# Four column quarters, group ends on TensorE and ScalarE, and a result made in quarters of 128 columns

## The chip, the cores and the metric

One core of a Trainium2 chip runs the whole kernel. The metric is the device time of one execution in microseconds (us); the median of the runs is used. All data is fp32. The engines are TensorE (PE; its weight loads are listed apart as PEld), VectorE (DVE), ScalarE (ACT), GpSimd (POOL) and SyncE (SP), whose queue issues all transfers here.

## The reference

A small conditional adapter: for each of 4 samples, two weight matrices are made from a vector `h` of 128 numbers, and then used on 1024 rows of `x`.

```python
# x (4, 1024, 512), h (4, 128); Wd (128, 512), Wu (512, 128); Wdd, Wdu (65536, 128)
dWd = ((h @ Wdd.T + bdd) * 0.1).reshape(B, 128, 512)
dWu = ((h @ Wdu.T + bdu) * 0.1).reshape(B, 512, 128)
Wd_b = Wd + dWd
Wu_b = Wu + dWu
down = relu(einsum('bld,bnd->bln', x, Wd_b) + bd)
up = einsum('bln,bdn->bld', down, Wu_b) + bu
return x + up
```

Wdd and Wdu are 33.5 MB each and are read once; x and the result are 8.4 MB each.

## The kernel before

**Chunks and groups.** Wdd and then Wdu are read in 32 chunks each of 2048 rows (1 MB), through a ring `w` of four. DVE transposes a chunk in 32x32 blocks into a ring `wt` of four (L240), in two instructions of 1024 elements a partition, each with a semaphore of its own, so that the matmuls can begin on the front half. TensorE multiplies it with `st`, a zero-filled pattern of `h` (`sum_chunk`, L406 to L417): four fp32 matmuls of 64 stationary columns and 512 moving ones, which go alternately to the lower and the upper 64 partitions of `acc`. Each fp32 matmul is two instructions in the trace. Four chunks make a group. A group ends so: ACT copies `acc` to `g_rows` with the factor 0.1 (`copy_group`, L324), TensorE transposes that in four steps into `gt` (`turn_group`, L425), and DVE adds the two halves and the base weights into `wd_b` or `wu_b` in two additions (`add_group`, L246 and L248). The eight groups of Wdd are "down" groups, those of Wdu "up" groups. Wd is transposed once on TensorE for `base_d` (L440, L334), Wu for `base_u` (L508, L368).

**The first stage** (loops `turn`) handles Wdd. **The second stage** (loop over `t` from 0 to 31, each engine has its own) handles Wdu, and each step t carries a share of the work on x. At t below 16 TensorE transposes x (`turn_x` twice, L458) into a ring of four banks; ACT copies them to `xt` (L349), POOL adds `bu` to x (L393). At t from 3 to 18 one `down_unit` (L468; eight instructions of 256 columns) computes 256 rows, and ACT applies bias and relu (L357, `copy_down`). From t = 19 on an `up_unit` (L481) multiplies two row tiles with 256 columns of `wu_b` into a bank, and DVE adds it to x two steps later (`finish_unit`, L290, `UP_LAG`), ahead of the next chunk's transpose in program order.

**Order.** The order on each engine is that of the program text. In a step TensorE does the chunk's sum, then at t % 4 = 1 `turn_group` for the group before, then `turn_x`, `down_unit`, `up_unit`. ACT does at t % 4 = 1 `copy_group`, then the copies of x, then `copy_down`. The left half (columns 0 to 255) of the result needs up groups 0 to 3 and is made in 16 units inside t = 19 to 31; the right half needs all groups and is made in 16 units after the last group has been added. SP loads a chunk when the one four before it is transposed; the stores (`store`, L186) lie between loads and after them.

Of the kernel before, what the change touches and what calls it, by code (L numbers as in the profile page):

```python
# [5 lines left out]
P = 128  # L6
QUAD = 32
# [18 lines left out]
FILL = SLOTS * (PART + Q * B)  # L26
FILL_STEP = PART + Q * B
# [11 lines left out]
HALF = D // 2  # L39
UP_I = 2  # L40
UP_UNITS = B * I // UP_I

# [3 lines left out]
UP_START = 19  # L46
UP_AT = {}
_v = 0
for _t in range(UP_START, CHUNKS):
    _n = 2 if _t % 4 == 2 else 1  # L50
    UP_AT[_t] = list(range(_v, min(_v + _n, UP_UNITS)))
    _v += _n
assert _v >= UP_UNITS
# [10 lines left out]
def hyper_adapter(nc, x, cond, Wd, bd, Wu, bu, Wdd, bdd, Wdu, bdu, out):  # L64
# [10 lines left out]
    with ctx:  # L75
# [17 lines left out]
        base_d = sb("base_d", [P, C, N])  # L93
        base_u = sb("base_u", [P, D])
# [9 lines left out]
        nat = [down[:, b, 0:C, :] for b in range(B)]  # L104
        wd_nat, bdd_nat, wu_nat, bdu_nat = nat
# [4 lines left out]
        bank = [pb(f"bank{n}", [P, UP_I * HALF]) for n in range(BANK_RING)]  # L110
# [13 lines left out]
        base_summed = sem("base_summed")  # L124
        base_turned = sem("base_turned")
        base_ready = sem("base_ready")
        wt_front_ready = sem("wt_front_ready")
        wt_ready = sem("wt_ready")
        chunk_summed = sem("chunk_summed")
        g_ready = sem("g_ready")  # L130
        g_turned = sem("g_turned")
        part1_added = sem("part1_added")
        group_added = sem("group_added")
# [11 lines left out]
        def unit_at(v):  # L145

            return v // UP_UNITS, v % UP_UNITS // (I // UP_I), v % (I // UP_I) * UP_I

        def unit_x(v):
            half, b, i0 = unit_at(v)  # L150
            return xs[:, b, i0:i0 + UP_I, half * HALF:(half + 1) * HALF]

        @block.sync
        def _(sp):
# [9 lines left out]
            def turn(it):  # L164
                for u in range(TURN_CHUNKS):
                    c = TURN_CHUNKS * it + u
                    load_chunk(c, wdd_chunks[c], u % W_RING)
                    if u == 1 and isinstance(it, int):
                        load_base_d()

            def load_base_d():
                sp.dma_start(wd_nat, Wd.rearrange("n (c d) -> n c d", c=C)).then_inc(base_d_loaded, 16)
                sp.dma_start(bdd_nat, bdd.rearrange("(n c d) -> n c d", c=C, d=P)).then_inc(base_d_loaded, 16)  # L173

            def load_base_u():
                sp.dma_start(wu_nat, Wu.rearrange("(c d) n -> d c n", c=C)).then_inc(base_u_loaded, 16)
                sp.dma_start(bdu_nat, bdu.rearrange("(c d n) -> d c n", c=C, n=N)).then_inc(base_u_loaded, 16)
                sp.dma_start(bu_all[:], bu.rearrange("(o d) -> o d", o=1).to_broadcast([P, D])
                             ).then_inc(base_u_loaded, 16)
                sp.dma_start(bd_col[:], bd.rearrange("(p o) -> p o", o=1)).then_inc(base_u_loaded, 16)  # L180

            def store(v, units):
                half, b, i0 = unit_at(v)
                i0 -= (units - 1) * UP_I
                sp.wait_ge(unit_final, v + 1)
                sp.dma_start(out_rows[b, :, i0:i0 + units * UP_I, half * HALF:(half + 1) * HALF],  # L186
                             xs[:, b, i0:i0 + units * UP_I, half * HALF:(half + 1) * HALF]
# [8 lines left out]
            at = {t: v for t, units in UP_AT.items() for v in units if v % 4 == 3}  # L196
            for t in range(CHUNKS):
# [4 lines left out]
                load_chunk(CHUNKS + t, wdu_chunks[t], t % W_RING)  # L202
                if t - UP_LAG - W_RING - 1 in at:
                    store(at.pop(t - UP_LAG - W_RING - 1), 4)
                    stores += 1
            for t in sorted(at):
                store(at[t], 4)
                stores += 1
            for v in range(UP_UNITS + 1, 2 * UP_UNITS - 2, 2):
                store(v, 2)  # L210
                stores += 1
            for v in range(2 * UP_UNITS - 2, 2 * UP_UNITS):
# [5 lines left out]
        def _(dve):  # L218
# [9 lines left out]
            for q in range(Q):  # L228
                rows = slice(QUAD * q, QUAD * (q + 1))
                place = st[rows].rearrange("p r (s z) -> p r s z", z=FILL_STEP)[:, :, :, q * B:(q + 1) * B]  # L230
                nc.vector.tensor_copy(place, h32[rows].unsqueeze(2).to_broadcast([QUAD, R, SLOTS, B])
                                      ).then_inc(st_ready, 1)

            def transpose(c, slot, tslot, loaded):
                dve.wait_ge(w_loaded[slot], loaded)
                if later(c, T_RING):
                    dve.wait_ge(chunk_summed, c - T_RING + 1)
                chunk = w[:, slot, :].rearrange("p (k r h) -> p k r h", r=R, h=QUAD)
                for r, ready in ((0, wt_front_ready), (R // 2, wt_ready)):
                    nc.vector.transpose(wt[:, tslot, r:r + R // 2].rearrange("p r (k j) -> p k r j", j=QUAD),  # L240
                                        chunk[:, :, r:r + R // 2]).then_inc(ready, 1)

            def add_group(g, parts, base, total):

                dve.wait_ge(g_turned, g + 1)
                nc.vector.tensor_tensor(total, parts[1], base, ALU.add).then_inc(part1_added, 1)  # L246
                dve.wait_ge(part1_added, g + 1)
                nc.vector.tensor_tensor(total, parts[0], total, ALU.add).then_inc(group_added, 1)  # L248

            def turned_parts():  # L250
                v = gt[:].rearrange("p c (a s b) -> p c a s b", s=SQ, b=B)
                return [v[:, :, a] for a in range(2)]

            def add_down_group(g):
                n = bass.ds(g * SQ, SQ)
                total = wd_b[:, :, :, n].rearrange("p c b s -> p c s b")
                base = base_d[:, :, n].unsqueeze(3).to_broadcast([P, C, SQ, B])
                add_group(g, turned_parts(), base, total)

            def add_up_group(g):  # L260
                d = slice((g - GROUPS) * D // GROUPS, (g - GROUPS + 1) * D // GROUPS)
                total = wu_b[:, :, d].rearrange("p b (s c) -> p c s b", c=C)
                base = base_u[:, d].rearrange("p (s c) -> p c s", c=C)
                add_group(g, turned_parts(), base.unsqueeze(3).to_broadcast([P, C, SQ, B]), total)

            def turn(it):
                for u in range(TURN_CHUNKS):
                    c = TURN_CHUNKS * it + u
                    transpose(c, u % W_RING, u % T_RING, 16 * (2 * it + u // W_RING + 1))
                    if u == 3 and isinstance(it, int):  # L270

                        dve.wait_ge(base_d_loaded, 16 * 2)
                        nc.vector.scalar_tensor_tensor(wd_nat, bdd_nat, DELTA_SCALE, wd_nat,
                                                       ALU.mult, ALU.add).then_inc(base_summed, 1)
                    if u == 3 and not isinstance(it, int):
                        add_down_group(2 * it - 1)
                    if u == SLOTS + 3:
                        if isinstance(it, int):
                            dve.wait_ge(base_ready, 1)
                        add_down_group(2 * it)  # L280
# [5 lines left out]
            def finish_unit(v):  # L286
                place = unit_x(v)
                dve.wait_ge(bu_added, v % UP_UNITS + 1)
                dve.wait_ge(up_summed, v + 1)
                nc.vector.tensor_tensor(place, bank[v % BANK_RING][:].rearrange("p (i d) -> p i d", d=HALF),  # L290
                                        place, ALU.add).then_inc(unit_final, 1)

            for t in range(CHUNKS):
                c = CHUNKS + t
                transpose(c, t % W_RING, t % T_RING, 16 * (c // W_RING + 1))
                if t == 2:
                    dve.wait_ge(base_u_loaded, 16 * 4)
                    nc.vector.scalar_tensor_tensor(wu_nat, bdu_nat, DELTA_SCALE, wu_nat,
                                                   ALU.mult, ALU.add).then_inc(base_summed, 1)
                if t == 2 * SLOTS - 1:  # L300
                    dve.wait_ge(base_ready, 2)
                if t % SLOTS == 3:

                    g = c // SLOTS - 1
                    add_down_group(g) if g < GROUPS else add_up_group(g)
# [3 lines left out]
            for t in range(CHUNKS, CHUNKS + UP_LAG):  # L309
                if t == CHUNKS + UP_LAG - 1:  # L310
                    add_up_group(2 * GROUPS - 1)
                for v in UP_AT.get(t - UP_LAG, ()):
                    finish_unit(v)
            for v in range(UP_UNITS, 2 * UP_UNITS):
# [3 lines left out]
        def _(act):  # L318
            def copy_group(g, n):

                act.wait_ge(chunk_summed, SLOTS * (g + 1))
# [5 lines left out]

            def turn(it):
                for u in range(TURN_CHUNKS):
                    if u == 1 and not isinstance(it, int):  # L330
                        copy_group(2 * it - 1, 1)
                    if u == 5 and isinstance(it, int):
                        act.wait_ge(base_turned, 1)
                        nc.scalar.activation(base_d[:], bank[0][:].rearrange("p (c n) -> p c n", c=C),  # L334
                                             ACT.Copy).then_inc(base_ready, 1)
                    if u == SLOTS + 1:
                        copy_group(2 * it, 0)
# [23 lines left out]
            for t in range(CHUNKS):  # L361
# [4 lines left out]
                if t == SLOTS + 1:  # L366
                    act.wait_ge(base_turned, 2)
                    nc.scalar.activation(base_u[:], gt[:].rearrange("p c n -> p (c n)"), ACT.Copy  # L368
                                         ).then_inc(base_ready, 1)
# [7 lines left out]
            copy_group(2 * GROUPS - 1, 1)  # L377

        @block.gpsimd
        def _(pool):  # L380
# [8 lines left out]
            bu_pair = bu_all[:].unsqueeze(1).to_broadcast([P, UP_I, D])  # L389
# [149 lines left out]
```

## Time and profile before

| | |
|---|---|
| median of 3 runs | 245.08 us (244.66 to 245.51) |
| the profiled execution's own time | 245.09 us |
| its span in the trace | 243.2 us |
| PE busy | 215.1 us, 88% |
| DVE busy | 189.4 us, 78% |
| ACT, POOL busy | 34.9 us, 39.8 us |
| bytes moved | 85.35 MB, mean 351 GB/s |

The span runs from the first to the last record of the profiled execution; what lies around it is 245.09 - 243.2 = 1.9 us. A share of busy time is a mean over stages with different limits, so the stages have to be read one by one.

### The profile page before, as it was taken

How to read it: one execution, taken by the hardware profiler on the slowest of the kernel's cores; microseconds unless marked ns; L12 is line 12 of the kernel's file. 1: busy time of each engine (PE TensorE's matmuls, PEld its weight loads, DVE VectorE, ACT ScalarE, POOL GpSimd, SP SyncE). 2: the span in 40 equal slices, each digit the busy share in tenths (PEclk: the TensorE clock that was granted, in tenths of full speed). 3: DMA queues.
4: the chain of work that ended last, by engine and by line, in shares of the span. 5: the costliest groups of instructions: out<-in, count | busy, mean ns of one | idle time of the engine just before them, and what ended most of it. 6: DMA issues, size and time to landing. Idle time of an engine off the chain costs nothing.

```text
span 243.2 us, 2728 instructions
## 1 busy us (share of the span) xinstructions
PE 215.1 (88%) x972; PEld 98.0 (40%) x972; DVE 189.4 (78%) x200; ACT 34.9 (14%) x67; POOL 39.8 (16%) x23
## 2 busy tenths in 40 slices
PE   0798797878979796989999999999999999997991
PEld 0213121212212122446556655665644535354881
DVE  2799999899999994887377775295178999985782
ACT  2001000000000000412442333324110000000000
POOL 2000000000000000666444553465000000000000
PEclk9999999999999997999999999999999999999998
DMA  5999999999999999999999999949335889950897
GB/s 220 426 420 425 426 415 422 420 419 391 377 350 425 426 410 384 426 416 423 423 420 423 416 423 416 410 168 388 163 147 222 327 268 360 386 191 0 286 337 242
DMA packets 20419, 85.35 MB, mean 351 GB/s; under 512 B 1588, under 2 KB 10808, under 8 KB 11192
## 3 DMA queue, kind: packets, MB, share of 16 engines
q1 hardware_dynamic: 20408, 85.21, 88.6%
q8 instruction: 7, 0.11, 0.2%
q14 instruction: 4, 0.03, 0.0%
HBM read 76.81 MB, written 8.39 MB: 350 GB/s over the span
## 4 chain that ended last, share of the span: by engine, by line
PE 52%; DVE 19%; DMA 17%; issue 6%; ACT 2%; SPq 1%; DVEq 0%; ACTq 0%
PE acc L414 21%; DVE wt L240 17%; PE bank L481 12%; PE dn L468 12%; DMA w<-in_L_cond_Wdd_dram 11%; DMA w<-in_L_cond_Wdu_dram 6%; PE bank L458 5%; PE gt L425 2%; DVE wd_b L246 1%; ACT xt L349 1%; SPq L158 1%; ACT g_rows L324 1%; ACT down L357 0%; SPq L173 0%; DVE xs L290 0%
## 5 line engine op out<-in xcount | busy, mean ns | idle before, releaser
L240 DVE STREAM_TRANSPOSE wt<-w 128x1024 f32<-128x1024 f32 x128 | 149.2, 1214 | 25.4 <-DMA w<-in_L_cond_Wdu_dram 19.8
L414 PE MATMUL acc<-wt,st 128*64 128x512 f32 x512 | 132.1, 624 | 18.2 <-DVE wt L240 16.6
L414 PEld LDWEIGHTS acc<-wt,st 128*64 128x64 f32 x512 | 29.6, 138 | 96.0 <-DVE wt L240 60.8
L393 POOL TENSOR_TENSOR xs<-xs,bu_all 128x1024 f32<-128x1024 f32 x16 | 38.0, 2377 | 128.9 <-PE bank L458 128.9
L481 PE MATMUL bank<-wu_b,down 128*128 128x256 f32 x128 | 31.1, 388 | 1.4 <-DVE wu_b L248 1.4
L468 PE MATMUL dn<-xt,wd_b 128*128 128x256 f32 x128 | 30.5, 381 | 0.0
L481 PEld LDWEIGHTS bank<-wu_b,down 128*128 128x128 f32 x128 | 23.2, 190 | 12.3 <-issue 5.7
L290 DVE TENSOR_TENSOR xs<-bank,xs 128x512 f32<-128x512 f32 x32 | 21.7, 681 | 7.3 <-PE bank L481 7.3
L349 ACT ACTIVATE xt<-bank 128x512 f32<-128x512 f32 x32 | 17.5, 594 | 64.5 <-PE dn L468 44.0
L468 PEld LDWEIGHTS dn<-xt,wd_b 128*128 128x128 f32 x128 | 23.1, 190 | 4.1 <-issue 1.6
L324 ACT ACTIVATE g_rows<-acc 128x512 f32<-128x512 f32 x16 | 9.6, 599 | 93.2 <-PE acc L414 93.2
L458 PEld LDWEIGHTS bank<-ident,xs 128*128 128x128 f32 x128 | 14.6, 146 | 10.5 <-issue 10.5
L458 PE MATMUL bank<-ident,xs 128*128 128x128 f32 x128 | 18.0, 285 | 0.0
L246 DVE TENSOR_TENSOR wu_b<-gt,base_u 128x256 f32<-128x256 f32 x8 | 4.8, 603 | 13.4 <-PE gt L425 13.4
L425 PEld LDWEIGHTS gt<-ident,g_rows 128*128 128x128 f32 x64 | 6.8, 141 | 13.2 <-issue 8.1
L425 PE MATMUL gt<-ident,g_rows 128*128 128x128 f32 x64 | 10.5, 286 | 0.7 <-ACT g_rows L324 0.4
L357 ACT ACTIVATE down<-dn,bd_col 128x256 f32<-128x256 f32 x16 | 7.6, 477 | 8.8 <-PE dn L468 8.8
L248 DVE TENSOR_TENSOR wu_b<-gt,wu_b 128x256 f32<-128x256 f32 x8 | 4.9, 617 | 0.3
L248 DVE TENSOR_TENSOR wd_b<-gt,wd_b 128x256 f32 (+1 forms) x8 | 4.9, 612 | 0.3
L246 DVE TENSOR_TENSOR wd_b<-gt,base_d 128x256 f32 (+1 forms) x8 | 4.6, 570 | 0.0
L334 ACT ACTIVATE base_d<-bank 128x512 f32<-128x512 f32 x1 | 0.6, 599 | 19.8 <-PE bank L440 19.8
L402 PE MATMUL gt<-ident,xt 4*128 4x4 f32 x4 | 0.6, 248 | 2.9 <-DVE xt L221 2.9
(19 smaller groups left out, 9.5 us busy)
## 6 DMA issues: line engine op xcount, KB each, us to landing
w<-in_L_cond_Wdd_dram SPq DMA_DIRECT2D x32, 1024.0 KB, 7.3
w<-in_L_cond_Wdu_dram SPq DMA_DIRECT2D x32, 1024.0 KB, 10.0
xs<-in_x_dram SPq DMA_DIRECT2D x8, 1024.0 KB, 14.6
out_dram<-xs SPq DMA_DIRECT2D x4, 1024.0 KB, 7.1
out_dram<-xs SPq DMA_DIRECT2D x7, 512.0 KB, 3.9
out_dram<-xs SPq DMA_DIRECT2D x2, 256.0 KB, 3.6
down<-in_L_cond_Wd_dram SPq DMA_DIRECT2D x1, 256.0 KB, 7.1
down<-in_L_cond_bdd_dram SPq DMA_DIRECT2D x1, 256.0 KB, 7.3
```

Source lines behind the costliest of these rows:

```text
L240: nc.vector.transpose(wt[:, tslot, r:r + R // 2].rearrange("p r (k j) -> p k r j", j=QUAD), chunk[:, :, r:r + R // 2]).then_inc(ready, 1)
L246: nc.vector.tensor_tensor(total, parts[1], base, ALU.add).then_inc(part1_added, 1)
L248: nc.vector.tensor_tensor(total, parts[0], total, ALU.add).then_inc(group_added, 1)
L290: nc.vector.tensor_tensor(place, bank[v % BANK_RING][:].rearrange("p (i d) -> p i d", d=HALF), place, ALU.add).then_inc(unit_final, 1)
L324: nc.scalar.activation(g_rows[:, n].rearrange("p (j k) -> p j k", k=K), acc[n][:].rearrange("p (k j) -> p j k", k=K), ACT.Copy, scale=DELT ...
L349: nc.scalar.activation(xt[:, j % XT_RING, c0:c0 + BANK_C, :], bank[m % BANK_RING][:].rearrange("p (c l) -> p c l", c=BANK_C), ACT.Copy).th ...
L393: nc.gpsimd.tensor_tensor(xs[:, b, i0:i0 + UNIT_I], xs[:, b, i0:i0 + UNIT_I], bu_pair, ALU.add).then_inc(bu_added, 1)
L414: last = nc.tensor.matmul(a[PART * part:PART * (part + 1)], st[:, r, s * PART:(s + 1) * PART], wt[:, slot, r], start=s == 0 and r < 2, sto ...
L425: last = nc.tensor.transpose(gt[:, k], g_rows[:, n, k * P:(k + 1) * P], ident[:])
L458: last = nc.tensor.transpose(bank[m % BANK_RING][:, n * P:(n + 1) * P], xs[:, b, i0 + i, c * P:(c + 1) * P], ident[:])
L468: last = nc.tensor.matmul(dn[:], wd_b[:, c, j // BATCH_UNITS], xt[:, j % XT_RING, c], start=c == 0, stop=c == C - 1)
L481: last = nc.tensor.matmul(bank[v % BANK_RING][:, i * HALF:(i + 1) * HALF], down[:, b, i0 + i], wu_b[:, b, half * HALF:(half + 1) * HALF], ...
```

## The change

- `sum_chunk` becomes `sum_pair`: `st` has 32 columns instead of 64, and the matmuls of two chunks (4 x 2, of 512 moving columns each) go in turn to four strips of 32 partitions of `acc`. TensorE waits for both chunks of a pair; DVE's transpose waits for a pair, too. The transpose of a chunk is one instruction of 2048 elements.
- A group's end leaves DVE. `turn_group` is now four times two accumulating fp32 matmuls with 64 moving columns: `g_rows` against `fold` (two identities added, which sums the two parts), and the base weights against a repeated slice of the identity. ACT copies `gt` to `wd_b` or `wu_b` (`store_group`), right behind `copy_group` in its order. The separate transposes of Wd and Wu and their copies go; Wd is read with whole rows of 2 KB.
- The result is made in quarters of 128 columns. A unit is four row tiles of 128 columns (same bank size). Quarter 0 runs at t = 16 to 19, two units a step; quarter 1 at t = 20 to 27, one a step; quarter 2 at t = 28 to 31, two a step; quarter 3, eight units, after the last group. Stores follow; their rows are 512 bytes.
- Chunks are read in the order 0, 2, 1, 3 within a group.

```diff
+PAIR = 2
+TILE = 32
+FILL = PAIR * (TILE + Q * B)
+FILL_STEP = TILE + Q * B
+ORDER = (0, 2, 1, 3)
...
-HALF = D // 2
-UP_I = 2
-UP_UNITS = B * I // UP_I
+QUARTERS = 4
+QD = D // QUARTERS
+UP_I = 4
+BATCH_UPS = I // UP_I
+UP_UNITS = B * BATCH_UPS
+ALL_UPS = QUARTERS * UP_UNITS
...
-UP_START = 19
...
+UP_AT = {16 + n: [2 * n, 2 * n + 1] for n in range(4)}
+UP_AT |= {20 + n: [UP_UNITS + n] for n in range(8)}
+UP_AT |= {28 + n: [2 * UP_UNITS + 2 * n, 2 * UP_UNITS + 2 * n + 1] for n in range(4)}
...
             def transpose(c, pair, slot, tslot, loaded):
                 dve.wait_ge(w_loaded[slot], loaded)
                 if later(c, T_RING):
+                    dve.wait_ge(pair_summed, pair - T_RING // PAIR + 1)
+                nc.vector.transpose(wt[:, tslot].rearrange("p r (k j) -> p k r j", j=QUAD),
+                                    w[:, slot, :].rearrange("p (k r h) -> p k r h", r=R, h=QUAD)
+                                    ).then_inc(wt_ready, 1)
...
+            def store_group(g, total):
+
+                act.wait_ge(g_turned, g + 1)
+                nc.scalar.activation(total, gt[:, :, 0:PART].rearrange("p c (s b) -> p c s b", b=B), ACT.Copy
+                                     ).then_inc(group_ready, 1)
...
                     copy_group(g, g % 2)
...
+                    down_group(g) if g < GROUPS else up_group(g)
...
+            def sum_pair(c, low, slot, a):
+
+                pe.wait_ge(wt_ready, c + PAIR)
                 for r in range(R):
+                    for h in range(PAIR):
+                        place = 2 * (r % 2) + h
+                        last = nc.tensor.matmul(a[TILE * place:TILE * (place + 1)],
+                                                st[:, r, low * TILE:(low + 1) * TILE], wt[:, slot + h, r],
+                                                start=low == 0 and r < 2, stop=low == 1 and r >= 2)
+                last.then_inc(pair_summed, 1)
+
+            def turn_group(g, n, base, select):
 
                 pe.wait_ge(g_ready, g + 1)
                 if later(g, 1):
+                    pe.wait_ge(group_ready, g)
                 for k in range(C):
-                    last = nc.tensor.transpose(gt[:, k], g_rows[:, n, k * P:(k + 1) * P], ident[:])
+                    nc.tensor.matmul(gt[:, k, 0:PART], g_rows[:, n, k * P:(k + 1) * P], fold[:],
+                                     start=True, stop=False)
+                    last = nc.tensor.matmul(gt[:, k, 0:PART], base(k),
+                                            select(k).unsqueeze(2).to_broadcast([P, SQ, B]),
+                                            start=False, stop=True)
                 last.then_inc(g_turned, 1)
...
             def up_unit(v):
-                half, b, i0 = unit_at(v)
-                pe.wait_ge(group_added, GROUPS + (half + 1) * GROUPS // 2)
+                quarter, b, i0 = unit_at(v)
+                pe.wait_ge(group_ready, GROUPS + (quarter + 1) * GROUPS // QUARTERS)
...
-                sum_chunk(c, s, t % T_RING, acc[n][:])
+                if s % PAIR == 0:
+                    sum_pair(c, s // PAIR, t % T_RING, acc[n][:])
```

## Rows read from the trace of the kernel before

**Rows 1.** The page: engines' busy time, transfer rate in 40 slices of 6.1 us.
```profile
PE 215.1 (88%) x972; PEld 98.0 (40%) x972; DVE 189.4 (78%) x200; ACT 34.9 (14%) x67; POOL 39.8 (16%) x23
GB/s 220 426 420 425 426 415 422 420 419 391 377 350 425 426 410 384 426 416 423 423 420 423 416 423 416 410 168 388 163 147 222 327 268 360 386 191 0 286 337 242
```

**Rows 2.** Stretches: from:to, length; busy time of PE, PEld, DVE, ACT, POOL; PEclk, DMA share, GB/s.
```profile
70.00:80.00 10.00, 8.51 (x38) 2.09 (x36) 9.97 (x11) 0.60 (x1) 0.00 (x0) 1.00 1.00 422
120.00:130.00 10.00, 10.00 (x54) 6.13 (x52) 7.85 (x8) 2.90 (x6) 5.49 (x3) 1.00 1.02 425
190.00:200.00 10.00, 10.00 (x44) 4.39 (x42) 9.99 (x12) 0.60 (x1) 0.00 (x0) 1.00 0.81 276
```

**Rows 3.** Groups with shapes: line, engine, out<-in, count | busy us, mean ns | idle before.
```profile
L240 DVE STREAM_TRANSPOSE wt<-w 128x1024 f32<-128x1024 f32 x128 | 149.2, 1214 | 25.4 <-DMA w<-in_L_cond_Wdu_dram 19.8 <-DMA w<-in_L_cond_Wdd_dram 3.6 <-PE acc L414 1.1
L246 DVE TENSOR_TENSOR wu_b<-gt,base_u 128x256 f32<-128x256 f32 x8 | 4.8, 603 | 13.4 <-PE gt L425 13.4
```

**Rows 4.** DVE in order of time: start, us, instructions [idle before]; start of Wdd's middle and of stage two.
```profile
49.69 9.13 DVE L240 STREAM_TRANSPOSE wt<-w 128x1024 f32<-128x1024 f32 x8
59.87 2.36 DVE L240 STREAM_TRANSPOSE wt<-w 128x1024 f32<-128x1024 f32 x2
...
91.95 2.37 DVE L240 STREAM_TRANSPOSE wt<-w 128x1024 f32<-128x1024 f32 x2 [1.29 <-DMA w<-in_L_cond_Wdu_dram]
111.85 4.86 DVE L240 STREAM_TRANSPOSE wt<-w 128x1024 f32<-128x1024 f32 x4 [1.66 <-DMA w<-in_L_cond_Wdu_dram]
```

**Rows 5.** The chain that ended last, in order of time: start, us, what.
```profile
110.65 1.87 PE acc L414 x8
112.52 1.02 PE bank L458 x8
113.54 1.74 PE dn L468 x8
...
117.85 0.66 PE gt L425 x4
118.51 0.87 PE bank L458 x8
...
137.71 0.87 PE bank L458 x8
...
168.77 1.87 PE acc L414 x8
170.64 1.92 PE dn L468 x8
...
182.41 1.06 PE bank L481 x4
...
188.85 0.86 PE bank L481 x4
...
224.16 14.09 PE bank L481 x64
...
238.35 0.69 DVE xs L290
```

**Rows 6.** The first weight loads of the last burst, two narrow windows: start, union of times, count.
```profile
224.16 0.19 PEld L481 LDWEIGHTS bank<-wu_b,down 128*128 128x128 f32 x1 [1.59 <-DVE wu_b L248]
224.16 0.30 PEld L481 LDWEIGHTS bank<-wu_b,down 128*128 128x128 f32 x2 [1.59 <-DVE wu_b L248]
```

**Rows 7.** ACT beside TensorE around t = 17, in order of time: start, us, instruction.
```profile
172.60 0.47 ACT L357 ACTIVATE down<-dn,bd_col 128x256 f32<-128x256 f32 x1 [2.28 <-PE dn L468]
172.97 0.59 ACT L324 ACTIVATE g_rows<-acc 128x512 f32<-128x512 f32 x1
```

**Rows 8.** Stretches as in rows 2: rates of 512-byte and 1 KB rows, and the clock.
```profile
91.00:92.00 1.00, 0.00 (x0) 0.00 (x0) 0.04 (x1) 0.00 (x0) 0.00 (x0) 1.00 1.12 308
95.00:96.00 1.00, 1.00 (x4) 0.00 (x0) 0.00 (x0) 0.00 (x0) 0.00 (x0) 0.50 0.99 410
230.00:232.00 2.00, 2.00 (x11) 1.77 (x10) 1.66 (x3) 0.00 (x0) 0.00 (x0) 1.00 1.02 345
```

More of the change, by code:

```diff
@@ L102, in hyper_adapter @@
         cond_rep = xt[0:B, 0, 1:3, :].rearrange("b c (r q i) -> b (c r) q i", q=Q, i=QUAD)
-        nat = [down[:, b, 0:C, :] for b in range(B)]
-        wd_nat, bdd_nat, wu_nat, bdu_nat = nat
+        bdd_nat = down[:, 0, 0:C, :].rearrange("p c n -> p (c n)")
+        bdu_nat = down[:, 1, 0:C, :]
         acc = [pb(f"acc{n}", [P, COLS]) for n in range(2)]
@@ L201, in _ @@
                     load_base_u()
[L202 to L209, printed above, removed]
+                load_chunk(CHUNKS + t, wdu_chunks[t // SLOTS * SLOTS + ORDER[t % SLOTS]], t % W_RING)
+                for v in UP_AT.get(t - UP_LAG - W_RING - 1, ()):
+                    if v % BATCH_UPS == BATCH_UPS - 1:
+                        store(v, BATCH_UPS)
+                        stores += 1
+            for t in range(CHUNKS - UP_LAG - W_RING - 1, CHUNKS):
+                for v in UP_AT.get(t, ()):
+                    if v % BATCH_UPS == BATCH_UPS - 1:
+                        store(v, BATCH_UPS)
+                        stores += 1
+            for v in range(ALL_UPS - UP_UNITS + 1, ALL_UPS - 2, 2):
                 store(v, 2)
                 stores += 1
-            for v in range(2 * UP_UNITS - 2, 2 * UP_UNITS):
+            for v in range(ALL_UPS - 2, ALL_UPS):
                 store(v, 1)
@@ L230, in _, with transpose @@
                 place = st[rows].rearrange("p r (s z) -> p r s z", z=FILL_STEP)[:, :, :, q * B:(q + 1) * B]
-                nc.vector.tensor_copy(place, h32[rows].unsqueeze(2).to_broadcast([QUAD, R, SLOTS, B])
+                nc.vector.tensor_copy(place, h32[rows].unsqueeze(2).to_broadcast([QUAD, R, PAIR, B])
                                       ).then_inc(st_ready, 1)
-            def transpose(c, slot, tslot, loaded):
+            def transpose(c, pair, slot, tslot, loaded):
                 dve.wait_ge(w_loaded[slot], loaded)
@@ L236, in transpose @@
                 if later(c, T_RING):
[L237 to L248, printed above, removed]
@@ L326, in copy_group, with down_group, up_group @@
                                      ACT.Copy, scale=DELTA_SCALE).then_inc(g_ready, 1)
-            def turn(it):
[L329 to L337, printed above, removed]
+            def store_group(g, total):
+                act.wait_ge(g_turned, g + 1)
+                nc.scalar.activation(total, gt[:, :, 0:PART].rearrange("p c (s b) -> p c s b", b=B), ACT.Copy
+                                     ).then_inc(group_ready, 1)
+            def down_group(g):
+                store_group(g, wd_b[:, :, :, bass.ds(g * SQ, SQ)].rearrange("p c b s -> p c s b"))
+            def up_group(g):
+                d = slice((g - GROUPS) * D // GROUPS, (g - GROUPS + 1) * D // GROUPS)
+                store_group(g, wu_b[:, :, d].rearrange("p b (s c) -> p c s b", c=C))
+            def turn(it):
+                for n in range(2):
+                    if n == 1 or not isinstance(it, int):
+                        copy_group(2 * it + n - 1, 1 - n)
+                        down_group(2 * it + n - 1)
             turn(0)
@@ L377, in _ @@
             copy_group(2 * GROUPS - 1, 1)
+            up_group(2 * GROUPS - 1)
         @block.gpsimd
@@ L404, in _ @@
             last.then_inc(cond_turned, 1)
-            def sum_chunk(c, s, slot, a):
-                pe.wait_ge(wt_front_ready, c + 1)
+            def sum_pair(c, low, slot, a):
+                pe.wait_ge(wt_ready, c + PAIR)
                 for r in range(R):
-                    if r == R // 2:
-                        pe.wait_ge(wt_ready, c + 1)
-                    part = r % 2
-                    last = nc.tensor.matmul(a[PART * part:PART * (part + 1)],
-                                            st[:, r, s * PART:(s + 1) * PART], wt[:, slot, r],
-                                            start=s == 0 and r < 2, stop=s == SLOTS - 1 and r >= 2)
-                last.then_inc(chunk_summed, 1)
@@ new lines, in turn_group, with turn_down_group, turn_up_group @@
+                    last = nc.tensor.matmul(gt[:, k, 0:PART], base(k),
+                                            select(k).unsqueeze(2).to_broadcast([P, SQ, B]),
+                                            start=False, stop=True)
+                last.then_inc(g_turned, 1)
+            def turn_down_group(g, n):
+                turn_group(g, n, lambda k: base_d[:, k * P:(k + 1) * P],
+                           lambda k: ident[:, bass.ds(g * SQ, SQ)])
+            def turn_up_group(g):
+                first = (g - GROUPS) * D // GROUPS
+                row = first % P
+                pick = ident[:, row:row + D // GROUPS].rearrange("p (s c) -> p c s", c=C)
+                turn_group(g, g % 2, lambda k: base_u[:, first // P], lambda k: pick[:, k])
@@ L434, in turn @@
                         pe.wait_ge(g_ready, 2 * it + n - 1)
-                    sum_chunk(c, s, u % T_RING, acc[n][:])
-                    if u == 4 and isinstance(it, int):
-                        pe.wait_ge(base_summed, 1)
-                        for k in range(C):
-                            last = nc.tensor.transpose(bank[0][:, k * P:(k + 1) * P], wd_nat[:, k], ident[:])
-                        last.then_inc(base_turned, 1)
+                    if s % PAIR == 0:
+                        sum_pair(c, s // PAIR, u % T_RING, acc[n][:])
                     if u == 1 and not isinstance(it, int):
-                        turn_group(2 * it - 1, 1)
+                        turn_down_group(2 * it - 1, 1)
                     if u == SLOTS + 1:
-                        turn_group(2 * it, 0)
+                        if isinstance(it, int):
+                            pe.wait_ge(fold_ready, 1)
+                            pe.wait_ge(base_d_summed, 1)
+                        turn_down_group(2 * it, 0)
             turn(0)
@@ L480, in up_unit @@
                 for i in range(UP_I):
-                    last = nc.tensor.matmul(bank[v % BANK_RING][:, i * HALF:(i + 1) * HALF],
-                                            down[:, b, i0 + i], wu_b[:, b, half * HALF:(half + 1) * HALF],
+                    last = nc.tensor.matmul(bank[v % BANK_RING][:, i * QD:(i + 1) * QD],
+                                            down[:, b, i0 + i], wu_b[:, b, quarter * QD:(quarter + 1) * QD],
                                             start=True, stop=True)
@@ L502, in _ @@
                     up_unit(v)
-                if t == SLOTS:
-                    pe.wait_ge(base_summed, 2)
-                    pe.wait_ge(group_added, GROUPS)
-                    for k in range(C):
-                        last = nc.tensor.transpose(gt[:, k], wu_nat[:, k], ident[:])
-                    last.then_inc(base_turned, 1)
-            turn_group(2 * GROUPS - 1, 1)
-            for v in range(UP_UNITS, 2 * UP_UNITS):
+            turn_up_group(2 * GROUPS - 1)
+            for v in range(ALL_UPS - UP_UNITS, ALL_UPS):
                 up_unit(v)
```

115 lines of the change are left out of this document (38 added, 77 removed).

## The prediction

> **What bounds the kernel now.** I read the page's busy shares and slices first [rows 1], then stretches of the span, because shares mix stages [rows 2], then the groups by shape for durations [rows 3], and last DVE in order of time and the chain of waits for cadences [rows 4, 5]. Three stages show. In the first (to about 90 us) DVE is busy 9.97 of 10 us and TensorE waits for it; four chunks take 59.87 - 49.69 = 10.2 us on DVE, transposes and two additions together, while four chunks at 422 GB/s are 4.19 MB / 422 = 9.9 us [rows 2, 4]. DVE is just ahead of the transfers as the limit. In the second stage, from about 107 us, TensorE is busy 10.00 of 10 us [rows 2]: a step with x costs 1.87 (sum) + 1.02 + 1.74 = 4.63 us, and four steps with a group's end 137.71 - 118.51 = 19.2 us [rows 5]. Up to some 155 us the transfers run at 416 to 425 GB/s beside it and then fall [rows 1], so they are the second limit there. From 182 to 222 us TensorE and DVE are both full [rows 2]. The third stage is the right half: 14.09 us of matmuls, then 0.69 us of DVE, then 243.2 - 239.04 = 4.16 us until the last store is in [rows 5].
>
> **Sum of a pair.** Eight instructions of 512 columns take 1.87 us two at a time, so one round of two is 1.87 / 4 = 0.47 us [rows 5]. A pair has 16 instructions; four at a time that is four rounds, 1.87 us again, against 3.74 before. No row shows four strips at once. Bounds: 1.87 (each strip adds no time, as the second does) and 3.74 (only two at a time). I take 1.87, because the two that run at once in the trace have separate moving data too. The Trainium skill (TensorE: Matmul & The Clock Gate, Part 3) says that three column tiles measured 2.38 times one; scaled to four it would make an estimated pair of 2.2 us and add 0.3 us for each pair on the path. No row shows three.
>
> **Transpose and the group's end.** One transpose of 2048 elements in place of two of 1024: from the cadence, eight instructions in 9.13 us are 2.28 us a chunk [rows 4]; I take 2.3 with its handoff, bounds 2.1 and 2.4. DVE loses 2 x 0.6 us a group [rows 3]. On TensorE a group's end grows from 0.66 us to 16 weight loads with short matmuls. The second weight load of a burst starts 0.30 - 0.19 = 0.11 us after the first [rows 6], so I take 16 x 0.108 = 1.73 us, +1.07; bounds 0.9 (half that pitch) and 3.0 (0.19, the whole record, each). ACT's copy of 256 elements is like L357, 0.47 us [rows 7]; it is on the path only at the last group.
>
> **First stage.** With DVE at 4 x 2.3 = 9.2 us a group the transfers bind at 9.9. Before chunk 0 of Wdu come 34.5 MB of 1.049 MB: 36.2 / 0.422 = 85.7 us behind a start of 3.7 gives 89.4, against 91.95 [rows 4]: -2.5 us, bounds 0 and -2.5. TensorE's longer group end is covered by its idle time: 2 x 1.87 + 1.73 = 5.5 us in 9.9.
>
> **Second stage, t to 15.** Chunk t = 5 began on DVE at 111.85 after a wait for its transfer [rows 4]; 2.5 earlier and 2.3 of transpose put the pair of t = 4 at 111.7 on TensorE. From there TensorE binds. Four steps cost 19.2 less 2 x 1.87 (half their sums) and 1.07 more, and there is a stall that is new. At t % 4 = 1 TensorE did a sum of 1.87 us ahead of `turn_group`; now it goes straight to it, and waits for `copy_group`, which stands behind `copy_down` of the step before on ACT. From the end of the down matmuls (170.64 + 1.92 = 172.56) to the end of L324 (172.97 + 0.59) is 1.0 us [rows 5, 7]. Behind this wait are queued on TensorE the transposes of x and the down unit, for which ACT and POOL wait in turn. So 19.2 - 3.74 + 1.07 + 1.0 = 17.5 us: 111.7 + 3 x 17.5 = 164.2 at t = 16, where the kernel before stood at 168.77 [rows 5]. Transfers: six MB in four steps are 14.9 us, under 17.5.
>
> **t = 16 to 31.** A unit of four tiles is eight pairs of weight load and matmul with 128 columns. Its streaming time is half of 0.22 us each, 14.09 / 64 / 2 = 0.11; the weight loads' pitch is 0.11 too [rows 5, 6]. If both overlap, a unit costs 0.87 us as before [rows 5]. Bounds 0.87 and 8 x 0.19 = 1.52 (the record's length as pitch). I take 0.87, since the loads of `turn_x`, 128 columns as well though in transposes, hide behind 128 moving ones (0.87 for eight [rows 5]). Then t = 16: 1.87 + 1.92 + 1.73 = 5.5; t = 17: 1.1 (the stall with its handoff) + 1.73 + 1.74 + 1.73 = 6.3; t = 18: 5.5, at 181.5. From here a loop binds that no engine shows alone: the units of an even step on TensorE, DVE's `finish_unit` for them (0.69), which stands ahead of the transpose of the odd chunk (2.3), and the pair, which waits for that chunk. With 0.3 of handoffs that is 3.3, and a round of two steps costs 1.87 + 1.06 + 3.3 = 6.3 us; DVE alone needs 2 x (2.3 + 0.69) = 6.0. First pair of t = 20: 184.8; four rounds to t = 28: 210.0. t = 28 and 29: 3.8 + 1.73 + 1.73 = 7.3; t = 30 and 31: 3.8 + 1.7; at 222.8. Group end 1.73, ACT 0.6, handoff 0.1: 225.2.
>
> **The tail.** Eight units 8 x 0.87 + 0.2 = 7.2, DVE 0.7, last store 4.2 + 0.3: 237.6. The 0.3 is for rows of 512 bytes: the nearest stretch, with loads of such rows, has 308 GB/s, against 345 for rows of 1 KB in the stores [rows 8]; 256 KB take 0.85 us at the lower rate, so the stores just keep up with the units. Bounds 0 and +3 (a rate of about 200).
>
> **Sum.** 237.6 - 243.2 = -5.6: the tail gives -7.0, the start of the tail +1.0, the stores +0.3, rounded. With 1.9 us around the span the time is 239.5 us; the profiled execution, 245.09, stands at the median of the runs, 245.08.
>
> **Rivals.**
> 1. Slower: weight loads set the pace of the quarter units, as half the columns lie between two loads. Place: 8 units at t = 16 to 19, 4 on the loop's path at t = 20 to 27, 8 at t = 28 to 31, 8 in the tail: 28. At 0.19 us a pair a unit costs 0.65 more, +18.2, so 257.7. It decides from +0.2 a unit, 0.135 us a pair, on. For it: the record is 0.19 us long. Against: the pitch of 0.11 [rows 6]. The Trainium skill (TensorE: Matmul & The Clock Gate, Back-to-back issue gap) has 81 ns for a stream of load and matmul at 128 columns where matmuls alone have 56, a rule that speaks against these units; 25 ns more a pair would be an estimated +0.2 a unit and +5.6 in all, near no change. Chance 0.15, spread from 245 up.
> 2. Slower: only two strips run at once. A pair stays at 3.74 and the steps have gained +1.07 and the stall: 2 pairs in each of 3 rounds before t = 16, then 2, 4 and 2 pairs on the path are 14 x 1.87 = 26.2, so 265.7. Against it speaks that two do run at once. Chance 0.05.
> 3. The clock. TensorE had 0.50 at 95 us after the one long idle stretch around 91 [rows 8]; that is 1.2 GHz in place of 2.4. TensorE will idle in 2 to 3 us pieces throughout stage one and in the loop of t = 20 to 27. In stage one a doubled 5.5 us is 11 in 9.9, nearly covered. In the loop it adds up to 1.87 + 1.06 a round, 4 rounds, +11.7: 251. Half of it gives 245. Chance 0.10.
> 4. Better than forecast: the stall on ACT or the handoffs are hidden, 4 x 1.1 less: 235.1. Chance 0.07.
> 5. The gain is eaten by small terms (DVE's finishes, POOL beside DVE, slow stores) and the time stays within 0.3%: 0.05.
>
> **How the numbers follow.** The forecast, 239.5 with 236 to 243.5 around it, has the remaining 0.58. Low 235.5 takes in part of rival 4; high 251 takes in rivals 5, 3 and the lower part of 1. Left out: rival 2, the top of 1, times below 235.5, about 0.18. A measurement of this kernel tells about 0.3% from no change. Faster: 0.58 + 0.07 + 0.03 (mild forms of 1 and 3) = 0.68; same 0.07; slower 0.25.
>
> **What would show it.** Pair: 16 instructions of L414's successor in 1.9 us, or 3.7. Units: eight weight loads at 0.11 or 0.19 pitch; the tail's 64 matmuls in 7.1 us or up to 12. ACT: TensorE idle about 1.1 us ahead of `turn_group` at t = 5, 9, 13, 17. Loop: DVE busy near 10 of 10 us at t = 20 to 27 with rounds of 6.3 us. Stage one: the first chunk of Wdu on DVE at 89.5 us. Clock: 1.00 in the second stage. The forecast fails first if a unit costs over 1.07 us, or if the transfers with their 512-byte rows become the limit behind t = 24.

## The result

| | median us | range, runs | to the kernel before |
|---|---|---|---|
| before | 245.24 | 244.66 to 245.51, 4 | |
| changed | 256.97 | 254.9 to 258.32, 4 | 1.047 (95%: 1.039 to 1.056) |

The change makes the kernel 4.7% slower, where 239.5 us was forecast. The profiled execution of the changed kernel took 254.9 us, with a span of 253.0; it is the fastest of its runs. Every ratio here leaves out runs that took over 1.5% more than the fastest of the same kernel, and every median is over all runs.

The page of the changed kernel, where it answers [rows 1] (with TensorE's granted clock in tenths):

```profile
PE 189.2 (75%) x1284; PEld 117.4 (46%) x1284; DVE 170.2 (67%) x105; ACT 43.9 (17%) x81; POOL 38.7 (15%) x23
PEclk9995978879779795779999679979999999979998
GB/s 231 426 421 420 426 420 420 421 417 426 418 422 425 416 378 424 422 416 426 416 424 421 417 376 210 202 262 57 111 41 291 269 364 382 402 338 157 164 167 249
```

Both full engines lost work, TensorE 26 us and DVE 19 us, and the kernel still got slower: no engine is full any more. The transfer row shows where. From slice 24 to 29 (counted from 0; 152 to 190 us) the transfers are at 41 to 262 GB/s: the loads have run ahead as far as the rings allow and wait for a slot to come free. The kernel before has such a dip too (168, 388, 163, 147 GB/s [rows 1]), but it starts later and is shallower. Most single costs came out as forecast. Groups of the changed kernel, and lines of its chain of waits (start, us, what):

```profile
L244 DVE STREAM_TRANSPOSE wt<-w 128x2048 f32<-128x2048 f32 x64 | 147.4, 2307 | 52.5 <-DMA w<-in_L_cond_Wdu_dram 21.9 <-PE acc L388 21.4 <-DMA w<-in_L_cond_Wdd_dram 8.5
L301 ACT ACTIVATE wu_b<-gt 128x256 f32<-128x256 f32 x8 | 5.1, 635 | 44.6 <-PE gt L401 44.6
```

```profile
182.39 1.78 PE bank L467 x16
184.18 0.17 PE gt L399 x2
...
185.91 1.78 PE dn L454 x8
...
189.47 1.85 PE acc L388 x16
```

A pair's 16 instructions on four strips take 1.85 us, four rounds of 0.46; the sum had 1.87. Two quarter units take 1.78 us, 0.89 each; the sum had 0.87. A group's end takes 185.91 - 184.18 = 1.73 us, as in the sum. DVE's transposes, 2.3 us with the handoff, fit as well. The first chunk of Wdu reached DVE at 90.8 us (89.5 forecast, 91.95 before [rows 4]): less than half of the 2.5 us that the first stage was to give. DVE's idle 21.4 us behind `PE acc` (1.1 before [rows 3]) is the new thing: it stands still because TensorE does not get to its pairs.

The place is t = 9 of the second stage (starts in us; ACT beside TensorE), and the same instructions in stretches (columns as in [rows 2]):

```profile
137.26 1.89 PE L454 MATMUL dn<-xt,wd_b 128*128 128x256 f32 x8
139.25 1.09 ACT L327 ACTIVATE xt<-bank 128x512 f32<-128x512 f32 x2 [3.16 <-PE dn L454]
140.22 0.48 ACT L335 ACTIVATE down<-dn,bd_col 128x256 f32<-128x256 f32 x1
140.57 0.61 ACT L294 ACTIVATE g_rows<-acc 128x512 f32<-128x512 f32 x1
141.24 0.54 PE L399 MATMUL gt<-fold,g_rows 128*128 128x64 f32 x2 [2.08 <-ACT g_rows L294]
...
144.55 1.91 PE L444 MATMUL bank<-ident,xs 128*128 128x128 f32 x8
146.26 2.88 PE L454 MATMUL dn<-xt,wd_b 128*128 128x256 f32 x8
```

```profile
139.20:141.20 2.00, 0.00 (x0) 0.00 (x0) 0.54 (x1) 1.93 (x4) 0.66 (x1) 1.00 1.04 430
141.40:148.20 6.80, 6.80 (x29) 6.44 (x30) 1.58 (x1) 0.63 (x1) 1.65 (x1) 0.50 1.02 422
148.40:151.00 2.60, 2.60 (x21) 0.81 (x20) 0.00 (x0) 1.45 (x3) 0.49 (x1) 1.00 0.92 375
```

After the down unit TensorE is idle for 2 us, while ACT does two copies of x, the relu and the group's copy in a row. ACT's bracket says why the copies of x come so late: they waited 3.16 us for `PE dn`, the down unit itself. The code has it, in `copy_x`: with a ring of three for `xt`, the copies at step t wait for the down unit of step t. And right behind the idle stretch the granted clock is 0.50 (1.2 GHz in place of 2.4) for 6.8 us, in which TensorE is busy all the time at half its pace: the eight transposes of x take 1.91 us in place of 1.04.

### The profile page after: what moved, and what is told of

Its sections match the earlier page's. It is cut to its first block, busy times and chain, and to the rows that moved or that the text cites. A ratio compares the mean times of both kernels' runs of the same rounds, so it can differ in the third digit from the quotient of the medians.

```text
span 253.0 us, 3267 instructions
## 1 busy us (share of the span) xinstructions
PE 189.2 (75%) x1284; PEld 117.4 (46%) x1284; DVE 170.2 (67%) x105; ACT 43.9 (17%) x81; POOL 38.7 (15%) x23
## 4 chain that ended last, share of the span: by engine, by line
PE 45%; DMA 33%; DVE 13%; issue 4%; ACT 3%; SPq 1%; ACTq 0%; DVEq 0%
DMA w<-in_L_cond_Wdd_dram 26%; PE dn L454 12%; DVE wt L244 12%; PE acc L388 11%; PE bank L467 9%; DMA w<-in_L_cond_Wdu_dram 7%; PE bank L444 6%; PE gt L399 3%; PE gt L401 3%; ACT xt L327 1%; DVE xs L268 1%; ACT down L335 1%; SPq L161 1%; ACT g_rows L294 1%; SPq L177 0%
## 5 line engine op out<-in xcount | busy, mean ns | idle before, releaser
L244 DVE STREAM_TRANSPOSE wt<-w 128x2048 f32<-128x2048 f32 x64 | 147.4, 2307 | 52.5 <-DMA w<-in_L_cond_Wdu_dram 21.9
L388 PE MATMUL acc<-wt,st 128*32 128x512 f32 x512 | 78.8, 744 | 45.5 <-DVE wt L244 45.5
L388 PEld LDWEIGHTS acc<-wt,st 128*32 128x32 f32 x512 | 15.7, 125 | 85.6 <-issue 52.2
L467 PE MATMUL bank<-wu_b,down 128*128 128x128 f32 x256 | 31.6, 278 | 0.7 <-ACT wu_b L301 0.7
L399 PE MATMUL gt<-fold,g_rows 128*128 128x64 f32 x128 | 26.4, 290 | 7.5 <-ACT g_rows L294 5.3
L399 PEld LDWEIGHTS gt<-fold,g_rows 128*128 128x128 f32 x128 | 20.7, 204 | 19.7 <-issue 13.2
L401 PE MATMUL gt<-ident,base_u 128*128 128x64 f32 x64 | 13.8, 301 | 0.0
L401 PE MATMUL gt<-ident,base_d 128*128 (+1 forms) x64 | 12.4, 275 | 0.0
L401 PEld LDWEIGHTS gt<-ident,base_u 128*128 128x128 f32 x64 | 11.1, 216 | 0.0
L401 PEld LDWEIGHTS gt<-ident,base_d 128*128 128x128 f32 x64 | 9.8, 193 | 0.0
```

Of the source, the lines that this page charges most:

```text
L244: nc.vector.transpose(wt[:, tslot].rearrange("p r (k j) -> p k r j", j=QUAD), w[:, slot, :].rearrange("p (k r h) -> p k r h", r=R, h=QUAD) ...
L388: last = nc.tensor.matmul(a[TILE * place:TILE * (place + 1)], st[:, r, low * TILE:(low + 1) * TILE], wt[:, slot + h, r], start=low == 0 an ...
L399: nc.tensor.matmul(gt[:, k, 0:PART], g_rows[:, n, k * P:(k + 1) * P], fold[:], start=True, stop=False)
L401: last = nc.tensor.matmul(gt[:, k, 0:PART], base(k), select(k).unsqueeze(2).to_broadcast([P, SQ, B]), start=False, stop=True)
L467: last = nc.tensor.matmul(bank[v % BANK_RING][:, i * QD:(i + 1) * QD], down[:, b, i0 + i], wu_b[:, b, quarter * QD:(quarter + 1) * QD], st ...
```

## The experiments

**Theory A.** At odd steps no sum stands any more between a down unit and what waits for ACT. TensorE is idle 2.1 us at t = 5, 9, 13 and 0.8 us at t = 7, 11, 15, and the longer stretches let the clock fall. (The expectations below count 2.5 us; the trace has 2.13, 2.08 and 2.08.) **Theory B.** The loss comes from the quarters themselves: units of 128 columns, stores with rows of 512 bytes, additions on DVE.

**A ring of four for xt.** One line in the changed kernel.

```diff
-XT_RING = 3
+XT_RING = 4
```

> The changed kernel with a ring of four for xt instead of three, nothing else. Theory A: in the changed kernel ACT's copies of x at step t wait for the down unit of the same step (ring of three), so behind each down unit stand 1.1 us of copies, the relu and at t % 4 = 1 the group's copy; the sum that TensorE did meanwhile at every odd step is gone, and TensorE stands idle 2.5 us at t = 5, 9, 13 and 0.8 us at t = 7, 11, 15; the 2.5 us then let the clock fall to 0.50 (5 us lost). With four buffers the copies run ahead: the idle time at t % 4 = 1 falls to about 1.2 us, that at t % 4 = 3 goes, and the clock holds in t = 5 to 15: 257 - 3 x 1.2 - 3 x 0.8 - 5 = 246 us. Theory B (the 512-byte stores and the quarter units make the loss): no change, 257.

Measured 244.29 us, 12.7 less, against 246 expected; ratio to the kernel before 0.995 (0.991 to 0.999). One extra buffer takes away the whole loss. TensorE's clock is 1.00 from 120 to 190 us. Theory B is out as the main cause. The pairs of t = 4 and t = 16, and the stall at t = 9 between them:

```profile
114.70 1.92 PE L388 MATMUL acc<-wt,st 128*32 128x512 f32 x16
137.94 0.43 PE L399 MATMUL gt<-fold,g_rows 128*128 128x64 f32 x2 [1.05 <-ACT g_rows L294]
167.20 1.92 PE L388 MATMUL acc<-wt,st 128*32 128x512 f32 x16
```

Four steps take (167.20 - 114.70) / 3 = 17.5 us with a stall of 1.05, which are the prediction's own two figures (17.5 and 1.0). So for this stretch the prediction costed the kernel with a ring of four, and not the changed one. Of the 3.8 us by which the profiled run still misses the forecast, 3.0 are the late start of t = 4 (114.7 against 111.7).

**The group's copy two steps earlier**, on ACT; that of the last Wdd group in front of the loop.

```diff
+            copy_group(GROUPS - 1, 1)
             for t in range(CHUNKS):
...
                 if t % SLOTS == 1:
                     g = c // SLOTS - 1
-                    copy_group(g, g % 2)
                     down_group(g) if g < GROUPS else up_group(g)
+                if t % SLOTS == 3:
+                    copy_group(c // SLOTS, c // SLOTS % 2)
...
-            copy_group(2 * GROUPS - 1, 1)
```

> The changed kernel with copy_group moved on ACT two steps earlier, to t % 4 = 3 (that of the last Wdd group in front of the loop); ring of three for xt as before. Theory A: the group's 0.5 us copy and its place behind the relu leave TensorE's path, turn_group starts at once behind the down unit and its 1.8 us cover ACT's copies: idle time at t = 5, 9, 13 falls from 2.5 to 0.3 us, that of 0.8 us at t % 4 = 3 grows to about 1.3; the clock holds: 257 - 6.6 + 1.5 - 5 = 247 us. Theory B: 257.

Measured 242.64 us (0.989; 0.985 to 0.993), 14.3 less, more than the 10 expected. This reaches the same idle stretch from its other end, without a new buffer: `turn_group`'s 1.73 us now stand over most of ACT's copies. The clock is 1.00 from 110 to 210 us here too.

**The clock alone.** Extra matmuls inside the idle time, in front of the wait; nothing uses their result, which the group's matmuls overwrite. They go into `gt` because no PSUM is left for a tile of their own: the first form of this experiment (x3_fill) had one and gave no result.

```diff
-                pe.wait_ge(g_ready, g + 1)
                 if later(g, 1):
                     pe.wait_ge(group_ready, g)
+                if isinstance(g, int) and GROUPS <= g < GROUPS + 3:
+                    for _ in range(4):
+                        nc.tensor.matmul(gt[:, 0:2].rearrange("p c n -> p (c n)"), ident[:],
+                                         base_d[:, 0:UNIT_I * P], start=True, stop=True)
+                pe.wait_ge(g_ready, g + 1)
```

> The changed kernel with four extra matmuls of 256 columns (eight instructions, 1.7 us at the full clock) on TensorE in front of the wait of turn_group for groups 8, 9 and 10 (t = 5, 9, 13), inside its 2.5 us of idle time. They go into gt, which the group's own matmuls then overwrite, and nothing uses them. If the clock falls because of this idle time, it now stays at 1.00 at 141 to 148 and 165 to 169 us, and what these stretches cost, 5 us of the profiled execution, comes back: 252 us against 257. If the clock falls for another reason: 257 to 258.

Measured 249.79 us (1.019; 1.014 to 1.023), 7.2 less than the changed kernel (5 expected), by adding work. The same place in its trace:

```profile
138.47 1.89 PE L399 MATMUL gt<-base_d,ident 128*128 128x256 f32 x8
140.72 0.30 PEld L403 LDWEIGHTS gt<-fold,g_rows 128*128 128x128 f32 x2 [0.76 <-ACT g_rows L294]
...
142.55 1.04 PE L448 MATMUL bank<-ident,xs 128*128 128x128 f32 x8
```

and the stretch behind it (columns as in [rows 2]):

```profile
140.70:148.00 7.30, 7.28 (x56) 5.36 (x57) 2.91 (x2) 2.09 (x4) 2.36 (x1) 1.00 1.02 421
```

The wait for ACT is still there and as long, but TensorE is busy in most of it, and the clock stays at 1.00: 7.28 us now hold 56 matmuls where 6.80 held 29. So the clock is a cause of its own. Of the 14.3 us that the early copy takes away, the clock behind the three stalls makes about half (7.2), the waits themselves the rest.

**Both repairs.** Ring of four and early copy.

> The changed kernel with both: ring of four for xt and copy_group two steps earlier. Theory A: no idle time of ACT's making is left between t = 4 and 16, the clock holds: 257 - 3 x 2.5 - 3 x 0.8 - 5 = 242 us, and one or two less from the start of the stage: 241. Then the loop of finish, transpose and pair (6.3 us for two steps) and the tail are as in the changed kernel. Theory B: 257.

Measured 239.46 us (0.972; 0.963 to 0.980), 17.5 less than the changed kernel, against 241 to 242 expected. TensorE in 16 us of the second stage (the two stretches behind, to 164 us, look the same):

```profile
116.00:132.00 16.00, 16.00 (x113) 11.69 (x112) 9.24 (x4) 7.08 (x14) 9.49 (x4) 1.00 1.01 418
```

The pairs of t = 4 and t = 16 start at 113.6 and 162.1 us: 16.2 us for four steps, without a gap, against 19.2 before and 17.5 in the sum (1.0 of which was a stall). The time is that of the forecast, 239.5, but not by the forecast's terms; the agreement is luck. In the trace t = 4 starts 1.9 us later than in the sum (113.6 against 111.7), the steps to t = 16 take 4.0 less, those to t = 20 0.9 less, the loop 1.0 more (26.2 against 25.2) and the steps from t = 28 on 2.0 more (17.2 against 15.2); the clock falls at t = 24 and t = 28 there, which the fillers below take away.

**Control: the ring of four in the kernel before.**

> The kernel before with a ring of four for xt instead of three. There every step has a sum of 1.87 us between a down unit and what waits for ACT's copies, so the wait on the down unit of the same step cost at most 0.2 us at four steps: no change, 244.5 to 245.2 us. If the ring of three were a cost of its own, as it is in the changed kernel (12.7 us), it would show here too: 233 to 240.

Measured 243.42 us (0.993; 0.991 to 0.996). The ring of three costs the kernel before 1.5 us, more than the expected range allowed, and the changed kernel 12.7.

**The quarters alone**, in the kernel before: constants, steps of the units, stores and `up_unit` as in the changed kernel, the rest untouched.

> The kernel before with the result in quarters of 128 columns alone (units, their steps and the stores as in the changed kernel; sums, group ends and transposes as before). TensorE is full from 107 to 222 us there, so eight units moved from the tail into t = 16 to 31 save 7.1 us at the end and cost 7.1 in the stretch, and DVE gets eight more additions of 0.69 us where it is full as well: 245 to 248 us. If the move itself were the gain: 238. If quarter units or 512-byte stores were slow in themselves: over 250.

Measured 246.66 us (1.005; 1.003 to 1.007), 1.5 us slower than the kernel before in the same comparison. The tail is shorter (13.7 us from its first matmul to the end of the span, against 19.0), but it starts 8.1 us later (232.3 against 224.2): the units moved out of it lengthen a stretch in which TensorE is full.

**The quarters undone**, in the kernel with both repairs: halves of 256 columns from t = 19, sixteen units in the tail, rows of 1 KB.

> Pairs and group ends of the changed kernel, ring of four for xt and copy_group two steps earlier, but the result in halves as in the kernel before (units of 2 x 256 columns from t = 19, sixteen in the tail, stores with rows of 1 KB). The tail is 7.1 us longer, t = 16 to 18 lose six units of 0.89 and t = 28 to 31 three: about 2 us less than 7.1 stay if DVE's loop (6.2 us for two steps) binds as before in t = 20 to 31. So the quarters are worth between 0 and 5 us on top of the pairs: 239.5 to 244.5, at the likeliest 242.

Measured 236.44 us (0.963; 0.956 to 0.970). I expected quarters to be worth up to 5 us; by the medians they cost 3.0. That figure is rough: the four runs of each kernel spread (234.8 to 237.6 against 236.8 to 240.6). With a lag of three, below, the same comparison is clear. The reading behind the expectation was wrong. In the traces halves have their tail 5.9 us longer (18.2 against 12.3), but they reach t = 20 8.0 us earlier (173.8 against 181.8), since TensorE, which is full there, has no eight units of quarter 0 to make. From t = 20 on both kernels take about as long to the tail (42.5 and 43.4 us).

**A lag of three** steps for `finish_unit`, with quarters and with halves.

```diff
-UP_LAG = 2
+UP_LAG = 3
```

> Ring of four for xt and copy_group two steps earlier (239.5 us), and UP_LAG 3 instead of 2: DVE adds a unit three steps after TensorE made it. If the loop of units, finish, transpose and pair binds at t = 20 to 27 (6.2 us for two steps), DVE alone binds then, with 2 x (2.25 + 0.65) = 5.8: 4 to 6 rounds give 2 us, 237.5. If the transfers bind there (342 to 398 GB/s with stores among the loads), no change: 239.5.

> Pairs, group ends, ring of four, copy_group early, the result in halves (236.4 us), and UP_LAG 3. As with quarters (239.5 to 236.1), the finish of a unit no longer stands between it and the next pair's transpose: 2 to 3 us, so 234. If the loop in t = 20 to 31 is bound by other things with halves: 236.4.

Measured 236.08 us (0.959; 0.951 to 0.966) with quarters, 229.27 us (0.934; 0.932 to 0.937) with halves. The loop of finish, transpose and pair is real: without it 3.4 and 7.2 us go (2 and 2 to 3 expected). With halves a part of this is the clock again: with a lag of two TensorE waits 2.3 us for DVE at t = 24 and t = 28 and the pairs behind take 2.91 and 3.46 us in place of 1.85; with a lag of three no pair does. With halves this beats both kernels, by 6.6% and 10.8%. The same two stretches of both kernels, first quarters, then halves:

```profile
190.00:200.00 10.00, 9.10 (x78) 6.11 (x78) 8.69 (x7) 1.24 (x2) 0.00 (x0) 1.00 1.06 376
200.00:210.00 10.00, 6.84 (x36) 3.77 (x35) 8.40 (x7) 0.00 (x0) 0.00 (x0) 0.66 0.95 328
```

```profile
190.00:200.00 10.00, 9.54 (x66) 5.93 (x66) 10.00 (x9) 0.61 (x2) 0.00 (x0) 1.00 0.99 364
200.00:210.00 10.00, 8.84 (x55) 6.35 (x55) 4.80 (x7) 1.84 (x3) 0.00 (x0) 1.00 0.53 178
```

With halves DVE is full and the last transpose ends at 201.3 us. With quarters DVE has gaps at 190 to 210 us. DVE's lines there name what it waits for:

```profile
198.31 2.31 DVE L244 STREAM_TRANSPOSE wt<-w 128x2048 f32<-128x2048 f32 x1 [1.19 <-DMA w<-in_L_cond_Wdu_dram]
205.69 2.31 DVE L244 STREAM_TRANSPOSE wt<-w 128x2048 f32<-128x2048 f32 x1 [1.59 <-DMA w<-in_L_cond_Wdu_dram]
```

The chunks come late there, with stores among the loads, TensorE is idle, and its clock falls (0.66). The 6.8 us between these two kernels are clear of the spread (233.6 to 236.8 against 228.3 to 229.5). How much of them is the 512-byte rows, how much the eight more units and how much the clock, no run separates.

**Filling the loop's gaps.** Extra matmuls, whose result nothing uses, in front of the pair's wait at t = 20 to 28 or 30, once with quarters (lag two), once with halves (lag three).

> Ring of four for xt and copy_group early (239.5 us), with extra matmuls on TensorE in front of the wait for the pair: four of 256 columns (1.7 us) at t = 20, 24, 28, two at t = 22, 26, into the unused half of the bank of dn, once all down units are copied. They compute nothing that is used. If the clock's falls in the loop (3.4 us at 194 and at 208 us in the profile of the kernel without them) cost about 1.8 us each by a slow pair and a slow unit on the loop's path, 3.5 us come back: 236. If the loop is bound by DVE or transfers anyway: 239.5, or more by the extra work.

> As x11, with the extra matmuls in front of the pair's wait at t = 20 to 30 (1.7 us where t % 4 = 0, 0.85 us where it is 2), which compute nothing that is used. If the clock still costs something there, 1 to 3 us come back: 232. If DVE binds with a lag of three, the clock's falls are off the path: as x11, 234, or slower by up to 1.

Measured 236.56 us (0.966; 0.964 to 0.969) against 239.46 without: the clock's falls at t = 24 and t = 28 (pairs of 3.47 and 3.58 us) are gone, and 2.9 us with them, where 3.5 were expected. With halves and a lag of three it was 234.96 us (0.959; 0.957 to 0.962) against 229.27 without: 5.7 us slower. The clock was 1.00 there already and the gaps at most 0.5 us, so the fillers, 7.7 us of them, stood on the path. Filling helps where TensorE waits for long, and costs most of its length where it doesn't.

## Why the prediction was wrong

- **What bounds the kernel now:** right by stages, but the groups of the page were read for durations only. The ACT line of the copies of x, in the page of the kernel before, had the answer in its last column:

```profile
L349 ACT ACTIVATE xt<-bank 128x512 f32<-128x512 f32 x32 | 17.5, 594 | 64.5 <-PE dn L468 44.0
```

- **Sum of a pair, group's end, transposes, units:** right, to 0.02 us a piece (1.85, 1.73, 2.3, 0.89). Rivals 1 and 2 did not come true: a pair of load and matmul takes 1.78 / 16 = 0.11 us, the streaming time alone, so the weight loads hide. The Trainium skill (TensorE: Matmul & The Clock Gate, Back-to-back issue gap) has 81 ns for such a pair where matmuls alone have 56; this trace shows no such surcharge.
- **First stage:** it gave 1.1 us (90.84 against 91.95), within the bounds of 0 and 2.5 but not the 2.5 that the sum used.
- **Second stage, t to 15: the step that failed.** The term of 1.0 us for ACT left out the copies of x, which with a ring of three wait for the down unit of the same step, and the sum put nothing for the clock behind the stalls. The stall at t % 4 = 1 was put at 1.0 us, from the relu and the group's copy. Two copies of x stand in front of them (1.1 us more), and at t % 4 = 3 the same chain delays the next down unit by 0.8 us; the sum had nothing there. TensorE's idle time measured 2.1 and 0.8 us. Without clock effects four steps took 19.6 us, not 17.5. Three rounds make 6.2 us. With a ring of four the same four steps take 17.5.
- **Rival 3, the clock, was named at places that decided less.** It was priced for stage one and for the loop from t = 20. It fell at t = 9 and 13, behind the very stalls the sum had just introduced, for 3.3 and 1.6 us on the path (from pair to pair 14.6 and 12.9 us, where the round without a fall took 11.3), together 4.9. The start of the stage is a further loss: the pair of t = 4 began at 114.9 instead of 111.7 us. Of these 3.2 us, 1.5 are the transfers: chunk t = 5 came to DVE at 110.85 instead of 109.35. The other 1.7 are TensorE's: it had half clock from about 94 to 104 us and again from 108 to 111 (the pairs of t = 0 and t = 2 took 3.64 and 3.15 us) and waited 1.2 us for the group's copy at t = 1; how much of the 1.7 each of the two makes is open. In all 3.2 + 6.2 + 4.9 = 14.3, and t = 16 began at 178.5 us instead of 164.2.
- **The loop from t = 20:** 198.2 to 223.6 us for four rounds, 25.4, against 25.2 forecast. The step at t = 28 met a half clock (pair 3.46 us), +1.9 to the tail. The tail, 240.7 to 253.0, took 12.3 us against 12.4. No stall stood at t = 17, where two units cover it: -0.9. The whole span: 237.6 + 14.3 - 0.9 + 0.2 + 1.9 - 0.1 = 253.0.
- **The stores:** in the tail the transfers ran at 288 GB/s with all engines busy; 308 was used. It cost nothing that shows.
- **The tail's gain is none.** That "the tail gives -7.0" was right, and the terms for t = 16 to 31 were right to 2 us; but the sum never compared quarters against halves with the pairs already in. That comparison is 239.46 against 236.44: the quarters lose 3.0 us, and 6.8 with a lag of three. What the repaired kernels gain on the kernel before comes with the pairs and the group ends; no run separates these two.
- **Range:** 251 was too low because rival 3 and the size of the stall were treated as independent, while the one brings on the other.

## What to carry to other kernels

When work is made faster or moved, list what it covered. Here a sum of 1.87 us stood over 2 us of ACT's queue, and taking it away laid that queue bare. Read the "idle before, releaser" column of the engines that are not busy, too: a short ring showed there as 44 us of waiting that cost 1.5 us, and 12.7 once nothing covered it. Work moved out of a tail into a stretch that is bound by the same engine gained nothing here (246.66 against 245.16 us); test such a move apart from the other parts of a change.

## What was not expected of the hardware

- Of three idle stretches of 2.1 us between busy ones, two were followed by a granted clock of 0.50: at once at t = 9, and 1.2 us after TensorE had begun again at t = 13. It stayed there for 6.8 and 3.3 us in which TensorE was busy without a gap. Behind the stretch at t = 5 it stayed at 1.00. In the kernel before, with gaps of 1.2 to 1.3 us in its first stage, it stayed at 1.00 too.
- In the first stage of the changed kernel the clock was 0.83 in the mean over 30 to 90 us, at no cost that shows, since the transfers bound (418 GB/s with all their engines busy). What a fall costs depends on where it comes:

```profile
30.00:90.00 60.00, 43.24 (x288) 17.58 (x288) 52.94 (x23) 7.13 (x12) 0.00 (x0) 0.83 1.01 418
```

- The changed kernel's runs spread over 1.3%, those of the kernel before over 0.3%; the profiled run had its longest fall at one of the three stalls and none at the first. The mean granted clock of its four runs lay between 0.875 and 0.895, so the falls probably differ from run to run; only one run has a trace.
- Four column strips with 512 fp32 columns each run at once at no loss: 16 instructions in 1.85 us, where eight in two strips took 1.87 [rows 5]. The Trainium skill (TensorE: Matmul & The Clock Gate, Part 3) has a speedup of 2.38 for three column tiles; no run here has three.
